# Loading only the right half of each Toeplitz band and copying its lower left quarter on VectorE

## The chip, the cores and the metric

The kernel runs on one core of a Trainium2 chip. The metric is the device time of one execution in microseconds (us); lower is better.

## What the kernel computes

`x` has shape batch 128, time 128, features 512; `cond` has shape 128 x 512. A causal convolution over time, whose taps are the rows of `cond`, is followed by a gated recurrence, and then by a tanh recurrence:

```python
x_pad = pad(x, K - 1 zeros in front of time)            # K = 128 taps
conv  = conv_b + sum(x_pad[:, k:k + L, :] * cond[k] for k in range(K))
proj  = conv @ Wp + bp
b_t, c_t = softplus(proj[..., :64]), tanh(proj[..., 64:])
u     = x @ Ws + bs
state = decay * state + dt * b_t * u_t                  # over time
x     = x + (c_t * state) @ Wo + bo
xW    = x @ Wx + b
h     = tanh(h @ Wh + xW_t)                             # 128 steps over time
out   = x + h
```

This case is about the convolution. For each of the 512 features it is a product of a 128 x 128 lower triangular Toeplitz matrix with that feature's 128 x 128 slice of `x`.

## The kernel before

**Stages.** The 512 features are worked off in KC = 4 chunks of P = 128. Each chunk has a convolution (`convolution`, one fp32 matmul per feature, 128 x 128 by 128 x 128) and then a projection (`projection`: transposes of the convolved tile and products with `Wp`). After the fourth chunk comes the recurrence over time, which takes the rest of the run. Within a chunk, four features share a PSUM bank (PER_BANK = 4), so a chunk fills BANKS = 32 banks in turn in the four banks CONV; ScalarE copies the even ones to SBUF and VectorE the odd ones (`copy_conv`), and TensorE may refill a bank only after its copy.

**The ring.** The matmul operands of CH = 8 features make one load, called here a group, so that a chunk has 16 groups and the kernel 64. Groups go to the RING = 8 slots of `t_ring` (the Toeplitz bands) and `x_ring` (the slices of `x`). The array `hankel` in HBM has each feature's taps once, behind zeros; the entry of a band at partition r and column l is `hankel[r + l]`, so a band is read with overlapping rows, a step of one tap from a partition to the next. Features lie in pairs (the last index of `t_ring`), so that one contiguous run of a partition is 512 B for 64 columns and 1024 B for all 128.

**The quarters of a band.** N = 64. Seen as partition halves by column halves: the upper left quarter (partitions 0 to 63, columns 0 to 63) is zero, which VectorE writes once per slot by memset. The upper right quarter is one DMA (`row, column = 0, N`: 64 partitions, 128 KB, 256 runs of 512 B); the lower half, left and right together, is a second (`N, 0`: 64 partitions, 256 KB, 256 runs of 1024 B). A third DMA brings `x_ring` (512 KB, 4 KB in each of 128 partitions). Since the entry depends on r + l alone, the lower left quarter has the same numbers as the upper right one.

**Order.** SyncE issues all loads, three DMAs per group on one queue (`load_ring`). It issues groups 0 to 7 at once, with the small loads of `vec`, `Wo` and `Ws` behind group 1 and `Wp` behind group 7. After that the load of group q + 8 waits until the matmuls of group q are done (`conv_done`). So the first eight groups of chunks 2 to 4 are loaded while the chunk before is convolved and projected, and their last eight during their own convolution. TensorE waits per group on the one semaphore `ring_loaded[slot]`, raised by all three DMAs. VectorE's program begins with the eight memsets, then scales vectors and `Wo` (waiting on their loads), and then runs `copy_conv` and the additions after the projections (`add_proj`) chunk by chunk. At the start ScalarE's first copy waits for GpSimd's work on the weights (`weights_ready`).

Of the kernel before, what the change touches and what calls it, by code (L numbers as in the profile page):

```python
# [12 lines left out]
TIME = 128  # L13
D = 512
N = 64
P = 128
KC = D // P
RING = 8
CH = 8
PER_BANK = 4  # L20
BANKS = P // PER_BANK
# [3 lines left out]
VECTORS = KC + 5  # L25
PAIRS = BANKS // 2
LAG = 3
LOAD = 3 * 16
DMA = 16

# [6 lines left out]
def build(nc, x_rev, x_dtb, hankel, h0_t, vectors, Wp, Ws, Wo, Wx, Wh, b, out):  # L38
# [6 lines left out]
    with ctx:  # L45
        def sb(stack, name, shape, dt=F32):
            return stack.enter_context(nc.sbuf_tensor(name, shape, dt))

        def sem(name):
            return ctx.enter_context(nc.semaphore(name))  # L50

        bank = [ctx.enter_context(nc.psum_tensor(f"bank{i}", [P, 512], F32)) for i in range(8)]
        CONV, TURN, PROJ = bank[0:4], bank[4:6] + bank[0:2], bank[2:4] + bank[6:8]
# [21 lines left out]
        with ExitStack() as first:  # L75

            t_ring = sb(first, "t_ring", [P, RING, CH // 2, TIME, 2])
            x_ring = sb(first, "x_ring", [P, RING, CH, BATCH])
            conv = sb(first, "conv", [P, TIME, P])  # L80
# [38 lines left out]
        def f(ap):  # L119
            return ap.bitcast(F32)  # L120

        ring_loaded = [sem(f"ring_loaded{i}") for i in range(RING)]
        t_zero = sem("t_zero")
        conv_done = sem("conv_done")
        conv_copied_act = sem("conv_copied_act")
        conv_copied_dve = sem("conv_copied_dve")
# [49 lines left out]
        def groups(engine, body):  # L176

            body(0, 0, True, False)
            body(1, 1, True, False)
            with engine.Fori(1, GROUPS // 2 - 1) as pair:  # L180
                body(2 * pair, 0, False, False)
                body(2 * pair + 1, 1, False, False)
            body(GROUPS - 2, 0, False, False)
            body(GROUPS - 1, 1, False, True)

        def toeplitz(row, column, n):

            return bass.AP(hankel.tensor, 2 * (row + column) + n * (CH // 2 * 4 * P),
                           [[2, N], [4 * P, CH // 2], [1, 2 * (TIME - column)]])

        block = ctx.enter_context(nc.Block())

        @block.sync
        def _(sp):
            def load_wp(c):
                rows = bass.ds(c * P, P)
                sp.dma_start(wp_now[:], Wp[rows, :]).then_inc(wp_loaded, DMA)  # L200

            def load_ring(n, slot):
                for row, column in ((0, N), (N, 0)):
                    sp.dma_start(t_ring[row:row + N, slot, :, column:, :].rearrange("p j l i -> p j (l i)"),  # L204
                                 toeplitz(row, column, n)).then_inc(ring_loaded[slot], DMA)
                sp.dma_start(x_ring[:, slot], x_rev[:, bass.ds(n * CH, CH), :]).then_inc(ring_loaded[slot], DMA)

            for n in range(RING):
                load_ring(n, n)
                if n == 1:  # L210
                    sp.dma_start(vec[:], vectors).then_inc(vec_loaded, DMA)
                    sp.dma_start(wo_f[0:N, :], Wo).then_inc(ws_wo_loaded, DMA)
                    sp.dma_start(ws_f, Ws.rearrange("(c p) n -> p c n", p=P)).then_inc(ws_wo_loaded, DMA)
            load_wp(0)
            per_chunk = P // CH
            with sp.Fori(0, KC - 1) as c:
                for q in range(per_chunk):

                    sp.wait_ge(conv_done, BANKS * c + CH // PER_BANK * (q + 1))
                    load_ring(per_chunk * c + q + RING, q % RING)  # L220
                    if q == per_chunk - 1:

                        sp.wait_ge(proj_done, BANKS * (c + 1))
                        load_wp(c + 1)
            for q in range(per_chunk - RING):
                sp.wait_ge(conv_done, BANKS * (KC - 1) + CH // PER_BANK * (q + 1))
                load_ring(per_chunk * (KC - 1) + q + RING, q % RING)

            sp.wait_ge(conv_done, BANKS * KC)  # L230
            sp.dma_start(w_f[:], Wx.rearrange("(c p) n -> p c n", p=P)).then_inc(wx_loaded, DMA)

            def load_x(g, slot):
                sp.dma_start(x_f[:, slot], x_dtb[:, bass.ds(g * G, G), :].rearrange("(c p) t b -> p c t b", p=P))\
                  .then_inc(x_loaded[slot], DMA)

            load_x(0, 0)
            sp.dma_start(b_rows[:], b.partition_broadcast(P)).then_inc(late_loaded, DMA)
            sp.dma_start(h0_f[:], h0_t.rearrange("(c p) b -> p c b", p=P)).then_inc(late_loaded, DMA)

            sp.wait_ge(weights_ready, 3)
            sp.dma_start(w_f[:], Wh.rearrange("(c p) n -> p c n", p=P)).then_inc(wh_loaded, DMA)

            sp.wait_ge(b_ready, BANKS - 2)
            sp.wait_ge(last_b_ready, 2)
            load_x(1, 1)

            def stores_and_loads(g, par, first, last):
                if not (last or (isinstance(g, int) and g == GROUPS - 2)):

                    sp.wait_ge(x1_ready, KC * (g + 1))
                    load_x(g + 2, par)

                for s in range(0, G, 1 if last else G):
                    n = 1 if last else G
                    sp.wait_ge(out_ready, G * g + s + n)
                    sp.dma_start(out[:, bass.ds(g * G + s, n), :].rearrange("(c p) t b -> p c t b", p=P),
                                 x1_f[:, par, :, s:s + n]).then_inc(stored[par], DMA)

            groups(sp, stores_and_loads)  # L260
            sp.wait_ge(stored[0], DMA * (GROUPS // 2))
            sp.wait_ge(stored[1], DMA * (GROUPS // 2 - 1 + G))
# [208 lines left out]
        def _(dve):  # L471
# [16 lines left out]
            nc.vector.tensor_scalar(rates[:, 1:2], rates[:, 0:1], -1.0, 1.0, ALU.mult, ALU.add).then_inc(rate_step, 1)  # L488
            decay = rates[N:P, 1:2]

            def copy_conv(c):
                with dve.Fori(0, BANKS // 4) as i:
                    m = 4 * i
                    for k in (1, 3):
                        dve.wait_ge(conv_done, BANKS * c + m + k + 1)
                        nc.vector.tensor_copy(conv[:, :, bass.ds((m + k) * PER_BANK, PER_BANK)],
                                              CONV[k][:].rearrange("p (d l) -> p l d", d=PER_BANK))\
                          .then_inc(conv_copied_dve, 1)

            def add_proj(c, m, k):  # L500
                dve.wait_ge(proj_done, BANKS * c + m + k + 1)
                cols = bass.ds((m + k) * 512, 512)
                nc.vector.tensor_tensor(bc[:, cols], PROJ[k][:], bc[:, cols], ALU.add).then_inc(proj_added, 1)  # L503

            copy_conv(0)
            with dve.Fori(0, BANKS // 4) as i:
                for k in range(4):
                    dve.wait_ge(proj_done, 4 * i + k + 1)
                    nc.vector.tensor_scalar(bc[:, bass.ds((4 * i + k) * 512, 512)], PROJ[k][:],  # L510
                                            bp_c[:, k % 2:k % 2 + 1], None, ALU.add).then_inc(proj_added, 1)
            with dve.Fori(1, KC - 1) as c:
                copy_conv(c)
                with dve.Fori(0, BANKS // 4) as i:
                    for k in range(4):
                        add_proj(c, 4 * i, k)

            copy_conv(KC - 1)

            def soft_abs_even(q, slot):
# [115 lines left out]
        def _(pe):  # L637
            pe.wait_ge(ident_ready, 1)

            def convolution(c):  # L640

                for d in range(P):
                    slot, m = (d // CH) % RING, d // PER_BANK
                    if d % CH == 0:
                        pe.wait_ge(t_zero, slot + 1)
                        pe.wait_ge(ring_loaded[slot], LOAD * (P // CH // RING) * c + LOAD * (d // CH // RING + 1))
                    if d % PER_BANK == 0 and m >= 4:  # L650

                        if m % 2 == 0:
                            pe.wait_ge(conv_copied_act, BANKS // 2 * c + (m - 4) // 2 + 1)
                        else:
                            pe.wait_ge(conv_copied_dve, BANKS // 2 * c + (m - 4) // 2 + 1)
                    mm = nc.tensor.matmul(CONV[m % 4][:, bass.ts(d % PER_BANK, TIME)], x_ring[:, slot, d % CH],  # L656
                                          t_ring[:, slot, d % CH // 2, :, d % 2], start=True, stop=True)
                    if d % PER_BANK == PER_BANK - 1:
                        mm.then_inc(conv_done, 1)
# [20 lines left out]
            with pe.Fori(0, KC - 1) as c:  # L680
                convolution(c)
                projection(c)

                pe.wait_ge(proj_added, BANKS * (c + 1) - 2)
# [136 lines left out]
```

## Time and profile before

| | |
|---|---|
| time, median of 3 runs | 1267.18 us (1267.06 to 1269.96) |
| the profiled execution's own time | 1265.97 us |
| its span | 1264.2 us |
| TensorE busy | 1187.3 us (94%) |
| VectorE busy | 657.2 us (52%) |
| share of the 16 DMA engines taken by the one load and store queue | 37.5% |
| TensorE's mean granted clock | 0.98 |

The span runs from the first to the last instruction of the profiled execution, and its own time holds in addition what lies around it. Busy shares are means over stages that differ: the four convolutions and projections fill the first 307 us, the recurrence the rest.

### The profile page before, as it was taken

How to read it: one execution, taken by the hardware profiler on the slowest of the kernel's cores; microseconds unless marked ns; L12 is line 12 of the kernel's file. 1: busy time of each engine (PE TensorE's matmuls, PEld its weight loads, DVE VectorE, ACT ScalarE, POOL GpSimd, SP SyncE). 2: the span in 40 equal slices, each digit the busy share in tenths (PEclk: the TensorE clock that was granted, in tenths of full speed). 3: DMA queues.
4: the chain of work that ended last, by engine and by line, in shares of the span. 5: the costliest groups of instructions: out<-in, count | busy, mean ns of one | idle time of the engine just before them, and what ended most of it. 6: DMA issues, size and time to landing. Idle time of an engine off the chain costs nothing.

```text
span 1264.2 us, 17115 instructions
## 1 busy us (share of the span) xinstructions
PE 1187.3 (94%) x5888; PEld 950.0 (75%) x5888; DVE 657.2 (52%) x1022; ACT 504.6 (40%) x756; POOL 333.4 (26%) x179
## 2 busy tenths in 40 slices
PE   4589899998859999999999999999999999999997
PEld 4567758677427888888888888888888888888886
DVE  2135354443996555555554555555555555455553
ACT  1144352443664434344433344443434443334432
POOL 1000000001433443333443333344333344333330
PEclk9899999998889999999999999999999999999999
DMA  9994968938102223222223222222322222322201
GB/s 215 222 216 109 273 145 212 257 98 223 34 0 67 68 91 105 71 66 66 66 69 104 92 66 66 66 66 94 100 71 66 66 66 73 106 87 66 66 34 67
DMA packets 82485, 129.54 MB, mean 102 GB/s; under 512 B 4960, under 2 KB 40800, under 8 KB 82464
## 3 DMA queue, kind: packets, MB, share of 16 engines
q1 hardware_dynamic: 82464, 129.26, 37.5%
q8 instruction: 13, 0.21, 0.1%
q14 instruction: 8, 0.07, 0.0%
HBM read 95.69 MB, written 33.55 MB: 102 GB/s over the span
## 4 chain that ended last, share of the span: by engine, by line
PE 84%; SPq 5%; DVE 4%; DMA 3%; issue 2%; ACT 0%; POOL 0%; DVEq 0%; POOLq 0%; ACTq 0%
PE bank L725 9%; PE bank L733 9%; PE bank L734 9%; PE bank L719 9%; PE bank L718 9%; PE bank L737 9%; PE bank L677 7%; PE bank L656 5%; PE bank L761 4%; PE bank L669 4%; DMA x_ring<-x_rev 3%; SPq L204 3%; PE bank L708 2%; PE bank L709 2%; PE bank L700 2%
## 5 line engine op out<-in xcount | busy, mean ns | idle before, releaser
L324 POOL TENSOR_TENSOR x_lo<-x_f,x_hi 128x512 fp32r<-128x512 f32 x126 | 160.2, 1307 | 556.0 <-ACT x_hi L442 556.0
L453 ACT ACTIVATE h_f<-z_f 128x512 f32<-128x512 f32 x128 | 80.9, 632 | 346.6 <-DVE z_f L612 346.6
L616 DVE TENSOR_TENSOR hT_lo<-bank,hT_hi 128x512 fp32r<-128x512 f32 x128 | 88.5, 691 | 216.1 <-ACT hT_hi L457 216.1
L733 PE MATMUL bank<-wh_hi,hT_hi 128*128 128x512 f32 x512 | 200.5, 392 | 0.0
L734 PE MATMUL bank<-wh_lo,hT_hi 128*128 128x512 f32 x512 | 200.0, 391 | 0.0
L719 PE MATMUL bank<-wx_lo,x_hi 128*128 128x512 f32 x512 | 199.7, 390 | 0.0
L718 PE MATMUL bank<-wx_hi,x_hi 128*128 128x512 f32 x512 | 199.5, 390 | 0.0
L656 PE MATMUL bank<-t_ring,x_ring 128*128 128x128 f32 x1024 | 134.7, 292 | 44.9 <-DMA x_ring<-x_rev 36.2
L656 PEld LDWEIGHTS bank<-t_ring,x_ring 128*128 128x128 f32 x1024 | 128.7, 202 | 52.1 <-issue 38.5
L612 DVE TENSOR_TENSOR z_f<-bank,b_rows 128x512 f32<-128x512 f32 x128 | 88.5, 691 | 132.4 <-PE bank L737 128.5
L318 POOL TENSOR_TENSOR x_lo<-x_f,x_hi 128x2048 fp32r<-128x2048 f32 x32 | 147.9, 4621 | 21.8 <-PE bank L669 21.8
L725 PE MATMUL bank<-wx_hi,x_lo 128*128 128x512 f32 x512 | 144.6, 404 | 0.4 <-POOL x_lo L324 0.4
L677 PE MATMUL bank<-turned,wp_now 128*128 128x512 f32 x256 | 134.4, 615 | 10.9 <-DVE bc L503 10.2
L737 PE MATMUL bank<-wh_hi,hT_lo 128*128 128x512 f32 x512 | 136.9, 389 | 0.0
L733 PEld LDWEIGHTS bank<-wh_hi,hT_hi 128*128 128x128 f32 x512 | 96.1, 188 | 26.0 <-ACT hT_hi L457 6.2
L457 ACT CAST hT_hi<-bank 128x512 fp32r<-128x512 f32 x128 | 75.1, 587 | 94.7 <-PE bank L761 94.7
L669 PEld LDWEIGHTS bank<-ident,conv 128*128 128x128 f32 x512 | 63.4, 142 | 64.7 <-issue 64.7
L718 PEld LDWEIGHTS bank<-wx_hi,x_hi 128*128 128x128 f32 x512 | 96.2, 188 | 20.4 <-ACT x_hi L442 0.4
L737 PEld LDWEIGHTS bank<-wh_hi,hT_lo 128*128 128x128 f32 x512 | 96.1, 188 | 20.2
L719 PEld LDWEIGHTS bank<-wx_lo,x_hi 128*128 128x128 f32 x512 | 96.2, 188 | 20.0
L734 PEld LDWEIGHTS bank<-wh_lo,hT_hi 128*128 128x128 f32 x512 | 96.2, 188 | 19.7
L442 ACT CAST x_hi<-x_f 128x512 fp32r<-128x512 f32 x128 | 79.6, 622 | 77.2 <-DVE x_f L589 75.0
(67 smaller groups left out, 1418.0 us busy)
## 6 DMA issues: line engine op xcount, KB each, us to landing
x_ring<-x_rev SPq DMA_DIRECT2D x64, 512.0 KB, 12.5
x_f<-x_dtb SPq DMA_DIRECT2D x32, 1024.0 KB, 8.1
out<-x_f SPq DMA_DIRECT2D x31, 1024.0 KB, 5.3
t_ring<-hankel SPq DMA_DIRECT2D x64, 256.0 KB, 11.7
t_ring<-hankel SPq DMA_DIRECT2D x64, 128.0 KB, 11.1
w_f<-Wx SPq DMA_DIRECT2D x1, 1024.0 KB, 5.4
w_f<-Wh SPq DMA_DIRECT2D x1, 1024.0 KB, 5.0
out<-x_f SPq DMA_DIRECT2D x4, 256.0 KB, 2.3
```

The source lines that it names most:

```text
L318: nc.gpsimd.tensor_tensor(x_lo[:], x_f[:, par], f(x_hi[:]), ALU.subtract).then_inc(xlo_ready, 1)
L324: nc.gpsimd.tensor_tensor(x1_lo[:, c], x1_f[:, par, c], f(x1_hi[:, c]), ALU.subtract)\
L612: nc.vector.tensor_tensor(z_f[:], ZB[s % 2][:], b_rows[:], ALU.add).then_inc(zsum_ready, 1)
L656: mm = nc.tensor.matmul(CONV[m % 4][:, bass.ts(d % PER_BANK, TIME)], x_ring[:, slot, d % CH], t_ring[:, slot, d % CH // 2, :, d % 2], star ...
L669: mm = nc.tensor.transpose(TURN[m % 4][:, bass.ts(i, P)], conv[:, m * PER_BANK + i], ident[:])
L677: nc.tensor.matmul(PROJ[n % 4][:], wp_now[:, bass.ts(n % 2, P)], turned[:, n % 4], start=True, stop=True)\
L718: nc.tensor.matmul(z, x1_hi[:, k, s], wx_hi[:, k], start=(k == 0), stop=False)
L719: nc.tensor.matmul(z, x1_hi[:, k, s], wx_lo[:, k], start=False, stop=False)
L725: mm = nc.tensor.matmul(z, x1_lo[:, k, s], wx_hi[:, k], start=False, stop=stop and k == KC - 1)
L733: nc.tensor.matmul(z, hT_hi[:, k], wh_hi[:, k], start=False, stop=False)
L734: nc.tensor.matmul(z, hT_hi[:, k], wh_lo[:, k], start=False, stop=False)
L737: mm = nc.tensor.matmul(z, hT_lo[:, k], wh_hi[:, k], start=False, stop=stop and k == KC - 1)
```

## The change

Of each band only the right half (all 128 partitions, columns 64 to 127) is loaded, in one DMA of 256 KB with 512 runs of 512 B. VectorE then copies the upper right quarter (64 partitions, 4 x 128 numbers in each) into the lower left one (`fill_band`), once for each of the 64 groups. The upper left quarter stays the memset one. The shared semaphore is split in three: `t_loaded[slot]` (the band's DMA, waited for by VectorE), `xr_loaded[slot]` (waited for by TensorE) and `t_full` (raised by the copy, waited for by TensorE). In `copy_conv` VectorE copies the band of group n + 1 ahead of the odd bank of group n, and the band of the next chunk's first group stands behind the last bank.

```diff
-LOAD = 3 * 16
-        ring_loaded = [sem(f"ring_loaded{i}") for i in range(RING)]
+        t_loaded = [sem(f"t_loaded{i}") for i in range(RING)]
+        xr_loaded = [sem(f"xr_loaded{i}") for i in range(RING)]
+        t_full = sem("t_full")
...
-        def toeplitz(row, column, n):
-            return bass.AP(hankel.tensor, 2 * (row + column) + n * (CH // 2 * 4 * P),
-                           [[2, N], [4 * P, CH // 2], [1, 2 * (TIME - column)]])
+        def band(n):
+            return bass.AP(hankel.tensor, 2 * N + n * (CH // 2 * 4 * P), [[2, P], [4 * P, CH // 2], [1, 2 * N]])
...
             def load_ring(n, slot):
-                for row, column in ((0, N), (N, 0)):
-                    sp.dma_start(t_ring[row:row + N, slot, :, column:, :].rearrange("p j l i -> p j (l i)"),
-                                 toeplitz(row, column, n)).then_inc(ring_loaded[slot], DMA)
-                sp.dma_start(x_ring[:, slot], x_rev[:, bass.ds(n * CH, CH), :]).then_inc(ring_loaded[slot], DMA)
+                sp.dma_start(t_ring[:, slot, :, N:, :].rearrange("p j l i -> p j (l i)"), band(n))\
+                  .then_inc(t_loaded[slot], DMA)
+                sp.dma_start(x_ring[:, slot], x_rev[:, bass.ds(n * CH, CH), :]).then_inc(xr_loaded[slot], DMA)
...
+            def fill_band(c, n):
+                slot = n % RING
+                dve.wait_ge(t_loaded[slot], DMA * (P // CH // RING) * c + DMA * (n // RING + 1))
+                nc.vector.tensor_copy(t_ring[N:P, slot, :, 0:N, :].rearrange("p j l i -> p j (l i)"),
+                                      t_ring[0:N, slot, :, N:, :].rearrange("p j l i -> p j (l i)")).then_inc(t_full, 1)
+
             def copy_conv(c):
-                with dve.Fori(0, BANKS // 4) as i:
-                    m = 4 * i
-                    for k in (1, 3):
-                        dve.wait_ge(conv_done, BANKS * c + m + k + 1)
-                        nc.vector.tensor_copy(conv[:, :, bass.ds((m + k) * PER_BANK, PER_BANK)],
-                                              CONV[k][:].rearrange("p (d l) -> p l d", d=PER_BANK))\
-                          .then_inc(conv_copied_dve, 1)
+                for n in range(P // CH):
+                    if n + 1 < P // CH:
+                        fill_band(c, n + 1)
+                    m = 2 * n + 1
+                    dve.wait_ge(conv_done, BANKS * c + m + 1)
+                    nc.vector.tensor_copy(conv[:, :, bass.ts(m, PER_BANK)],
+                                          CONV[m % 4][:].rearrange("p (d l) -> p l d", d=PER_BANK))\
+                      .then_inc(conv_copied_dve, 1)
...
+            fill_band(0, 0)
             copy_conv(0)
+            fill_band(0, P // CH)
...
             with dve.Fori(1, KC - 1) as c:
                 copy_conv(c)
+                fill_band(c, P // CH)
...
                     if d % CH == 0:
                         pe.wait_ge(t_zero, slot + 1)
-                        pe.wait_ge(ring_loaded[slot], LOAD * (P // CH // RING) * c + LOAD * (d // CH // RING + 1))
+                        pe.wait_ge(t_full, P // CH * c + d // CH + 1)
+                        pe.wait_ge(xr_loaded[slot], DMA * (P // CH // RING) * c + DMA * (d // CH // RING + 1))
```

SyncE's program where its loop over the later loads begins, before the change (one group is the rows from one `conv_done` wait to the next; `t_ring` is the band, `x_ring` the slice of `x`):

```order
L204 ISA [waits conv_done]
L204 DMA t_ring<-hankel 64x4x128
L204 DMA t_ring<-hankel 64x4x256
L206 ISA
L206 DMA x_ring<-x_rev 128x1024
L219 REGISTER_ALU
```

The same place now:

```order
L200 ISA [waits conv_done]
L200 DMA t_ring<-hankel 128x4x128
L202 ISA
L202 DMA x_ring<-x_rev 128x1024
L215 REGISTER_ALU
```

Two issues per group stand where there were three.

VectorE's program behind the memsets, before the change (`turned` holds `Wo` here, `bank` is a convolution bank):

```order
L484 TENSOR_SCALAR turned<-turned,rates_e 64x512 [waits ws_wo_loaded]
L486 TENSOR_SCALAR turned<-turned,rates_e 64x512 [waits wo_scaled]
L488 TENSOR_SCALAR rates<-rates 128x1 [waits rate_step]
L492 UNCONDITIONAL_BRANCH
L492 ISA
L496 ISA [waits conv_done]
L496 COPY conv<-bank 128x128x4
```

The same place now:

```order
L480 TENSOR_SCALAR turned<-turned,rates_e 64x512 [waits ws_wo_loaded]
L482 TENSOR_SCALAR turned<-turned,rates_e 64x512 [waits wo_scaled]
L484 TENSOR_SCALAR rates<-rates 128x1 [waits rate_step]
L491 COPY t_ring<-t_ring 64x4x128 [waits t_loaded0]
L491 COPY t_ring<-t_ring 64x4x128 [waits t_loaded1]
L500 COPY conv<-bank 128x128x4 [waits conv_done]
L491 COPY t_ring<-t_ring 64x4x128 [waits t_loaded2]
L500 COPY conv<-bank 128x128x4 [waits conv_done]
```

The first band copy, on which TensorE's first matmul now waits, stands behind the scaling of `Wo`; from there on a band copy and a bank copy alternate.

VectorE's program at the end of the first chunk's convolution, now (before, the wait on `proj_done` followed the last bank copy directly):

```order
L500 COPY conv<-bank 128x128x4 [waits conv_done]
L491 COPY t_ring<-t_ring 64x4x128 [waits t_loaded7]
L500 COPY conv<-bank 128x128x4 [waits conv_done] x2
L491 COPY t_ring<-t_ring 64x4x128 [waits t_loaded0]
L513 UNCONDITIONAL_BRANCH
L513 ISA
L516 ISA [waits proj_done]
L516 TENSOR_SCALAR bc<-bank,vec 128x512
```

The band copy of the next chunk's first group now stands ahead of the first addition behind a projection.

## Rows read from the trace of the kernel before

**Rows 1.** The four convolutions as windows: length, busy us per engine, clock, DMA share.

```profile
core 0: us, PE busy (x) PEld busy (x) DVE busy (x) ACT busy (x) POOL busy (x), PEclk, DMA share, GB/s
8.45:74.27 65.82, 41.48 (x256) 38.06 (x256) 11.91 (x21) 9.68 (x18) 2.94 (x4) 0.87 1.09 225
116.76:151.34 34.58, 30.31 (x257) 29.35 (x256) 11.33 (x17) 9.37 (x16) 0.00 (x0) 1.00 0.97 244
193.83:227.39 33.56, 29.98 (x257) 29.22 (x256) 11.21 (x17) 9.37 (x16) 0.00 (x0) 1.00 0.96 251
269.89:307.04 37.15, 32.93 (x257) 31.70 (x255) 11.21 (x17) 9.36 (x16) 0.00 (x0) 0.91 0.83 202
```

**Rows 2.** TensorE's waits, 0 to 380 us: who for whom, total, times, longest.

```profile
PE bank L656 <- DMA x_ring<-x_rev: 36.2, 20, 8.5
```

**Rows 3.** TensorE's timeline, first convolution: start, length, what, idle before and releaser.

```profile
8.45 6.05 PE L656 MATMUL bank<-t_ring,x_ring 128*128 128x128 f32 x32 [8.45 <-DMA x_ring<-x_rev]
18.81 5.60 PE L656 MATMUL bank<-t_ring,x_ring 128*128 128x128 f32 x32 [4.31 <-ACT conv L357]
...
29.82 2.08 PE L656 MATMUL bank<-t_ring,x_ring 128*128 128x128 f32 x16 [1.88 <-DMA x_ring<-x_rev]
...
72.19 2.08 PE L656 MATMUL bank<-t_ring,x_ring 128*128 128x128 f32 x16 [2.23 <-DMA x_ring<-x_rev]
```

**Rows 4.** The same timeline, second and third convolution.

```profile
139.09 2.08 PE L656 MATMUL bank<-t_ring,x_ring 128*128 128x128 f32 x16 [0.33 <-DMA x_ring<-x_rev]
...
149.26 2.08 PE L656 MATMUL bank<-t_ring,x_ring 128*128 128x128 f32 x16 [1.32 <-DMA x_ring<-x_rev]
...
193.83 23.76 PE L656 MATMUL bank<-t_ring,x_ring 128*128 128x128 f32 x208
```

**Rows 5.** The same timeline, last convolution.

```profile
290.82 2.06 PE L656 MATMUL bank<-t_ring,x_ring 128*128 128x128 f32 x16 [0.82 <-issue]
...
298.85 5.90 PE L656 MATMUL bank<-t_ring,x_ring 128*128 128x128 f32 x32 [1.05 <-issue]
```

**Rows 6.** SyncE's issues, second convolution: start, length, DMAs.

```profile
120.57 0.45 SPq L206 DMA_DIRECT2D x_ring<-x_rev  x1
...
148.54 1.30 SPq L204 DMA_DIRECT2D t_ring<-hankel  x2
150.03 1.43 SPq L206 DMA_DIRECT2D x_ring<-x_rev  x1
151.74 1.30 SPq L204 DMA_DIRECT2D t_ring<-hankel  x2
```

**Rows 7.** DMAs: KB, us to landing; issued at 120.57, from 148.54, at 151.74.

```profile
x_ring<-x_rev SPq DMA_DIRECT2D x1, 512.0 KB, 4.8
...
x_ring<-x_rev SPq DMA_DIRECT2D x1, 512.0 KB, 12.5
t_ring<-hankel SPq DMA_DIRECT2D x1, 256.0 KB, 11.7
t_ring<-hankel SPq DMA_DIRECT2D x1, 128.0 KB, 11.1
...
t_ring<-hankel SPq DMA_DIRECT2D x1, 128.0 KB, 11.3
```

**Rows 8.** VectorE groups, 0 to 380 us: form, count | busy, mean ns | idle.

```profile
L496 DVE COPY conv<-bank 128x512 f32 x64 | 44.1, 691 | 120.5 <-PE bank L656 120.5
L563 DVE COPY s_f<-v_f 64x128 f32<-64x128 f32 x1 | 1.2, 1209 | 0.0
L484 DVE TENSOR_SCALAR turned<-turned,rates_e 64x512 f32<-64x512 f32 x1 | 0.7, 704 | 0.0
L486 DVE TENSOR_SCALAR turned<-turned,rates_e 64x512 f32<-64x512 f32 x1 | 0.5, 479 | 0.0
```

**Rows 9.** VectorE's timeline around the second convolution's start.

```profile
114.50 3.33 DVE L510 TENSOR_SCALAR bc<-bank,vec 128x512 f32 x4 [0.55 <-PE bank L677]
118.97 0.69 DVE L496 COPY conv<-bank 128x512 f32 x1 [1.15 <-PE bank L656]
```

## Prediction

> **What bounds the kernel now.** I first split the run into stages, because the change touches the loads of the four convolutions alone. Their windows [rows 1] last 65.8, 34.6, 33.6 and 37.2 us and hold the same 128 fp32 matmuls each. In all four the DMA engines are busy nearly throughout (share 0.83 to 1.09), VectorE for about 11 us. Next I asked what TensorE waits for: within the first 380 us 36.2 us of its idle time end with the landing of `x_ring`, the third DMA of a load [rows 2]. The timeline of TensorE shows the shape. In the first convolution, from group 5 on, each group waits for its own load: groups 5 and 15 start at 29.82 and 72.19 [rows 3], so the pace is 42.37 / 10 = **4.24 us per load**. In the second convolution it is (149.26 - 139.09) / 3 = **3.39 us** at the end [rows 4], in the last one (298.85 - 290.82) / 2 = **4.0 us** [rows 5]. Where the operands lie ready TensorE needs 23.76 us for 13 groups [rows 4], **1.83 us per group**, hence 16 x 1.83 + 0.2 for the tail = **29.5 us** for a convolution. So the convolutions are bound by their loads, the first wholly, the others in their second half, and 29.5 us is the floor under each.
>
> **What the change removes.** Each load shrinks from 896 KB to 768 KB and from three issues to two. How much time that is depends on which of the two band DMAs cost it. In a backlog, landings follow each other as the queue is worked off [rows 6, 7]. Of the load issued from 148.54 the 128 KB DMA lands at 148.54 + 11.1 = 159.6, the 256 KB one, issued half of 1.30 us later, at 149.2 + 11.7 = 160.9, `x_ring` at 150.03 + 12.5 = 162.5; the next 128 KB one lands at 151.74 + 11.3 = 163.0. So the three take about 0.5, 1.3 and 1.6 us, together 3.4, which is the pace just found. The 256 runs of 512 B take 0.5 us and the 256 runs of 1024 B 1.3: more than twice the time for twice the bytes. No row shows 512 B runs to all 128 partitions in one DMA. Its price is bounded by the nearest rows: at `x_ring`'s bytes per time 256 / 512 x 1.6 = 0.8 us; at the small DMA's price per run 2 x 0.5 = 1.0; at both band DMAs' bytes per time 1.8 x 256 / 384 = 1.2; at the larger one's price per run 2 x 1.3 = 2.6. I take 1.0, since runs of just this length have that row. A load then takes **2.65 us** where it took 3.4.
>
> A rule stands beside that price. The Trainium skill, SBUF — State Buffer, section Door 1, has partitions 0 to 63 on eight of SBUF's sixteen DMA ports and 64 to 127 on the other eight, so each old band DMA had half the ports and the new one has all. From its ceiling of 435 GB/s for all ports I estimate 0.6 us for the 128 KB DMA and 1.2 for the 256 KB one; the rows' 0.5 and 1.3 agree. By that rule the new DMA would take 0.6 us instead of my 1.0, a load 2.25, and the sum below would be 37 us instead of 31.8, or 1230 us.
>
> **First convolution.** Its loads go at 4.24 us, 1.26 times as slow as in the second for the same bytes. If that factor stays the new pace is 2.65 x 1.26 = 3.35; if it comes from the two half-width DMAs getting in each other's way, it goes and the pace is 2.65. Nothing in the rows decides, and I take the middle, **3.1 us**. The bounds are 2.65 and, by bytes alone, 4.24 x 768 / 896 = 3.63. Between the first load and the sixteenth lie 15 of them: 15 x (4.24 - 3.1) = **17.1 us** saved.
>
> **The other convolutions.** Here the last eight loads are issued during the convolution. In the second, which starts at 116.76, `x_ring` of the first such load is issued at 120.57 and lands 4.8 us later [rows 6, 7], 8.6 us into the convolution; with one issue less, some 7.5. Seven more follow, then the last group's 2.1 us: 7.5 + 7p + 2.1 for a pace p. At the old pace, with 8.6, that gives 8.6 + 23.7 + 2.1 = 34.4, against 34.58 in the row. At p = 2.65 it gives 28.2, below the floor of 29.5, so TensorE becomes the bound and the second and third convolution save 34.6 - 29.5 = **5.1** and 33.6 - 29.5 = **4.1 us**. The last one has lost more: its later loads come at 4.0 us. Its mean pace from the same formula is (37.15 - 2.1 - 8.6) / 7 = 3.8; times 2.65 / 3.4 this is 3.0, so 7.5 + 21 + 2.1 = 30.6, saving **6.5 us**.
>
> **What the change adds.** 64 copies on VectorE of 64 partitions x 512 fp32, SBUF to SBUF. The trace has no such copy. The nearest rows are `Wo`'s scalings of the same shape: 479 ns in place, 704 ns from the lower to the upper partitions [rows 8]; a fourfold smaller copy with 1209 ns is the upper bound. I take 0.6 us. Per group VectorE then has 0.69 (a bank copy, [rows 8]) + 0.6 = 1.3 of TensorE's 1.83 us, and the copies hide twice: behind `x_ring`, which lands 1.6 us after the band where loads bound, and behind the previous group's matmuls where TensorE bounds. That cover is gone if a copy takes over 1.83 - 0.69 = 1.14 us; at 1209 ns each of up to 64 groups would cost 0.07 us, some 4 us at most.
>
> Two places need a look because VectorE runs in order. At each later convolution's start the copy for its second group stands behind the last additions, which end at 114.50 + 3.33 = 117.83 [rows 9]; the copy ends at 118.4, and the second group is due at 116.76 + 1.83 = 118.59: no stall, but only 0.2 us of slack. At each convolution's end the copy for the next chunk's first group stands ahead of the additions. Its band lands about 1 us after the last `x_ring`, before the last group's matmuls are over, and the first addition of the chunk cannot start until a projection product is done. At the very start the first copy stands behind the scaling of `Wo`, so TensorE starts at about 15.5 instead of 8.45 [rows 3]. It then had to wait anyway, for ScalarE until 18.81 with two groups done; those two groups took it 6.05 us, and with the later start I expect group 2 at 20 to 21.5. From there it gains on loads that come every 3.1 us and has caught up by group 7. Cost on the path: nothing, and 2 us if the pace is near 2.65. For all of this together I charge 1 us.
>
> **Sum.** 17.1 + 5.1 + 4.1 + 6.5 - 1 = 31.8 us. The profiled execution took 1265.97, so it would be 1234.2; the median of the runs is 1.2 us higher, so I forecast **1235 us**. The projections and the recurrence only move earlier.
>
> **Rivals.**
> *A. The loads stop binding everywhere (chance 0.25).* The two half-width DMAs are what makes the queue slow, and full-width loads run at 2.65 us or below in the first convolution too. For it: the slow factor of 1.26 has no other visible cause. Against: `x_ring`, full width already, is most of a load. First convolution: 15 x (4.24 - 2.65) = 23.9, less 2 for the late start; last one at the floor, 7.7. With 5.1 and 4.1 this is 38.8 saved, 1228 us. If the pace falls to 2.4, the first gives 27.6 less 2, and 1225. The port rule named above speaks for this rival too: transfers that each use all ports have no half to crowd.
>
> *B. Bytes alone count, at each stage's old rate (0.20).* First 15 x (4.24 - 3.63) = 9.1; the others at paces 2.9, 2.9 and 3.26: 29.9, 29.9 and 32.4 us, saving 4.7, 3.7 and 4.7. Together 22, less 1: 1246 us. For it: the rates differ between stages though the mix does not.
>
> *C. Runs alone count (0.05).* A load has 256 + 256 + 128 runs before and 512 + 128 after. If a run's price doesn't hang on its length, nothing is saved and the copies are hidden: 1267 us. Against: 0.5 against 1.3 us for 256 runs.
>
> *D. Slower (0.06).* The place is the band's DMA: 512 runs at the 1024 B run's price take 2.6 us where both old ones took 1.8, 0.8 more per load. First: 15 x 0.8 x 1.26 = 15 us; the other three 7 x 0.8 = 5.6 each. Together 32, so 1299 us. It decides once the new DMA takes over 1.8 us, 1.8 times my price. Against: half of those runs are exactly the old small DMA, at 0.5.
>
> **How the numbers follow.** My forecast with paces between A and B has 0.44. The range is 1223 to 1250: A and B with their bounds lie inside, C and D outside, and so do mixes such as B with slow copies. Differences within 0.3% (3.8 us) cannot be told from none by a measurement of this kernel. C is the same, with a little of D's milder form: 0.05. D gives slower, 0.05. The rest is faster, 0.90.
>
> **What would show it.** In the new profile the third step is right if the first convolution's groups start 3.1 us apart, from 2.65 (A) to 3.6 (B). The second and third convolution should last 29.5 to 30 us with no wait for `x_ring`, the last 29.5 to 32.5. The band copies should show 0.48 to 0.70 us, with TensorE hardly ever released by them. VectorE's busy time should grow by 64 x 0.6 = 38 us. The band's DMA should land about 1.6 us ahead of `x_ring`; a gap near zero would expose the copy. The prediction fails if the band's DMA takes clearly more than 1.2 us, if TensorE's waits move onto the copies, or if TensorE's granted clock falls to half during a projection, which happened in convolutions with gaps (mean 0.87 and 0.91, [rows 1]) and not in those without.

## The result and the profile after

The change makes the kernel faster: 1217.54 us (1216.49 to 1217.91) against 1267.12 us (1265.07 to 1269.96), a ratio of 0.9599 with a 95% interval of 0.9547 to 0.965. The prediction was 1235 us with a range of 1223 to 1250. The sign was right, but the measured time lies below the range: the gain was 49.6 us instead of 32. The kernel before was timed again with each set of experiments: medians 1266.69 and 1265.00 us, single runs from 1258.67 to 1274.13. It varies more than the changed kernel, whose four runs lie within 1.5 us.

The four convolutions of the changed kernel as windows (length, busy us per engine, granted clock, DMA share, GB/s), beside [rows 1]:

```profile
core 0: us, PE busy (x) PEld busy (x) DVE busy (x) ACT busy (x) POOL busy (x), PEclk, DMA share, GB/s
12.03:43.51 31.48, 31.26 (x256) 30.67 (x256) 16.98 (x30) 9.37 (x16) 1.85 (x2) 1.00 1.07 360
86.03:115.37 29.34, 29.29 (x257) 29.09 (x256) 17.47 (x32) 9.36 (x16) 0.00 (x0) 1.00 0.94 314
157.74:186.99 29.25, 29.25 (x257) 29.06 (x256) 17.53 (x32) 9.37 (x16) 0.00 (x0) 1.00 0.95 314
229.36:258.54 29.18, 29.18 (x257) 28.98 (x255) 17.53 (x32) 9.37 (x16) 0.00 (x0) 1.00 0.67 221
```

The first convolution ends at 43.51 us instead of 74.27, the others last 29.2 to 29.3 us instead of 34.6, 33.6 and 37.2. That is 30.8 + 5.2 + 4.3 + 8.0 = 48.3 of the 49.5 us by which the span fell (1264.2 to 1214.7). In the first convolution the DMA engines moved 360 GB/s, up from 225.

The granted clock is at its upper level (2.4 GHz) in all four, where the first and last had means of 0.87 and 0.91, so the clock could be a second cause of the gain. The old rows speak against it. In the kernel before, first convolution:

```profile
46.37 3.78 PE L656 MATMUL bank<-t_ring,x_ring 128*128 128x128 f32 x16 [1.22 <-DMA x_ring<-x_rev]
50.72 2.08 PE L656 MATMUL bank<-t_ring,x_ring 128*128 128x128 f32 x16 [0.57 <-DMA x_ring<-x_rev]
```

The group at 46.37 ran at a granted clock of 0.51, that is at the lower level (1.2 GHz), and took 3.78 us instead of 2.08. The next group still had to wait 0.57 us for its load.

TensorE's timeline shows each convolution as one long row. Against [rows 3 to 5] the waits for single loads are gone:

```profile
12.03 31.48 PE L664 MATMUL bank<-t_ring,x_ring 128*128 128x128 f32 x256 [12.03 <-DVE t_ring L491]
...
86.09 29.28 PE L664 MATMUL bank<-t_ring,x_ring 128*128 128x128 f32 x256
...
157.74 29.25 PE L664 MATMUL bank<-t_ring,x_ring 128*128 128x128 f32 x256
...
229.36 29.18 PE L664 MATMUL bank<-t_ring,x_ring 128*128 128x128 f32 x256
```

The first is still 2.2 us longer than the others. The chain of waits shows its last two groups at the pace of the loads, 2.18 us apart instead of 1.83:

```profile
39.27 2.06 PE bank L664 x16
41.33 0.13 issue
41.45 2.05 PE bank L664 x16
```

The trace has the landings of `x_ring` for these groups at 39.2 and 41.4 us.

TensorE's waits up to 340 us (compare [rows 2]):

```profile
PE bank L664 <- DVE t_ring L491: 12.0, 1, 12.0
```

VectorE's groups up to 380 us (count, then busy us in all and mean ns of one), the bank copy and the new band copy:

```profile
L500 DVE COPY conv<-bank 128x512 f32<-128x512 f32 x64 | 44.3, 691 | 47.5 <-PE bank L664 47.5
L491 DVE COPY t_ring<-t_ring 64x512 f32<-64x512 f32 x64 | 27.8, 435 | 2.1
```

The 64 copies take 435 ns in the mean. After the first, TensorE is never released by one.

To see what a load costs, take SyncE's issues of one load and the next, issued while TensorE finishes the first convolution and landing after it:

```profile
38.59 0.38 SPq L200 DMA_DIRECT2D t_ring<-hankel  x1
39.18 1.04 SPq L202 DMA_DIRECT2D x_ring<-x_rev  x1
40.48 0.59 SPq L200 DMA_DIRECT2D t_ring<-hankel  x1
41.26 1.08 SPq L202 DMA_DIRECT2D x_ring<-x_rev  x1
```

and their times from issue to landing (first load, then the next):

```profile
x_ring<-x_rev SPq DMA_DIRECT2D x1, 512.0 KB, 9.1
t_ring<-hankel SPq DMA_DIRECT2D x1, 256.0 KB, 7.9
...
x_ring<-x_rev SPq DMA_DIRECT2D x1, 512.0 KB, 9.2
t_ring<-hankel SPq DMA_DIRECT2D x1, 256.0 KB, 8.6
```

The landings are 46.5 (band), 48.3 (`x_ring`), 49.1, 50.5. So the second load's band takes 0.8 us and its `x_ring` 1.4, a load **2.2 us**. The 1.8 us between the first two landings is an exception: for the loads issued at 20.70 and 24.48 the trace has the band and `x_ring` landing at 29.1 and 30.5, and at 33.5 and 34.8, two loads in 4.3 us. Read the same way, [rows 6, 7] gave 0.5 + 1.3 + 1.6 = 3.4, and the first convolution's pace was 4.24.

### The profile page after: what moved, and what is told of

Read it like the earlier page. It is cut to its first block, busy times and chain, and to the rows that moved or that the text cites. A ratio compares the mean times of both kernels' runs of the same rounds, so it can differ in the third digit from the quotient of the medians.

```text
span 1214.7 us, 16920 instructions
## 1 busy us (share of the span) xinstructions
PE 1170.6 (96%) x5888; PEld 939.4 (77%) x5888; DVE 685.1 (56%) x1086; ACT 504.8 (42%) x756; POOL 333.7 (27%) x179
## 4 chain that ended last, share of the span: by engine, by line
PE 93%; DVE 3%; issue 1%; DMA 0%; ACT 0%; POOL 0%; DVEq 0%; SPq 0%; POOLq 0%
PE bank L664 10%; PE bank L733 10%; PE bank L741 10%; PE bank L742 10%; PE bank L745 9%; PE bank L727 9%; PE bank L726 9%; PE bank L685 8%; PE bank L769 5%; PE bank L677 4%; PE bank L716 2%; PE bank L717 2%; PE bank L702 2%; PE bank L708 2%; DVE bc L539 1%
## 5 line engine op out<-in xcount | busy, mean ns | idle before, releaser
L664 PE MATMUL bank<-t_ring,x_ring 128*128 128x128 f32 x1024 | 119.0, 276 | 12.3 <-DVE t_ring L491 12.0
L664 PEld LDWEIGHTS bank<-t_ring,x_ring 128*128 128x128 f32 x1024 | 118.0, 190 | 14.6 <-issue 14.6
```

## The experiments

**What made the loads slow.** The load shrank by 14% in bytes and its time by 35% (from 3.4 us) to 48% (from 4.24). The theory that I formed from this: a DMA over partitions 0 to 63 or 64 to 127 alone is slow and also slows what runs beside it (width theory). The rivals: bytes, length of a run, number of DMAs. Four kernels tell them apart.

*Whole band in one full-width DMA*, more bytes than ever and no copy:

```diff
-                for row, column in ((0, N), (N, 0)):
-                    sp.dma_start(t_ring[row:row + N, slot, :, column:, :].rearrange("p j l i -> p j (l i)"),
-                                 toeplitz(row, column, n)).then_inc(ring_loaded[slot], DMA)
+                sp.dma_start(t_ring[:, slot].rearrange("p j l i -> p j (l i)"), band(n)).then_inc(ring_loaded[slot], DMA)
```

> The kernel before with the whole band in one DMA over all 128 partitions (512 KB, 512 runs of 1024 B, the zero quarter read from the zeros of hankel), no copy and no memset. A load has 1024 KB, more than before (896) and after (768). Width theory (what made the loads slow is that each old band DMA reached only half of the partitions): loads run at the changed kernel's bytes per time, 768 KB in 2.2 us, so 2.9 us each; the first convolution ends near 52 us instead of 74, the others near their floor; 1228 us (1222 to 1236). Bytes theory: 4.24 x 1024 / 896 = 4.85 us per load in the first convolution, total 1280 to 1290 us. Run length theory (1024 B runs are the dear ones): 2.6 + 1.3 = 3.9 us per load, 1250 to 1262 us.

Measured: 1231.12 us, a ratio of 0.9711 (0.9653 to 0.977) to the kernel before. Consecutive groups of the first convolution:

```profile
48.77 2.08 PE L653 MATMUL bank<-t_ring,x_ring 128*128 128x128 f32 x16 [0.71 <-DMA x_ring<-x_rev]
51.57 2.08 PE L653 MATMUL bank<-t_ring,x_ring 128*128 128x128 f32 x16 [0.72 <-DMA x_ring<-x_rev]
```

1024 KB in 2.8 us, where 896 KB took 4.24: the width theory's number, and neither rival's. Bytes and run length can't be what held the loads back. They are not without effect once every DMA is full width: with 256 KB less per load the changed kernel is another 13.6 us faster.

*The right half in two DMAs of 64 partitions*, in the changed kernel:

```diff
-                sp.dma_start(t_ring[:, slot, :, N:, :].rearrange("p j l i -> p j (l i)"), band(n))\
-                  .then_inc(t_loaded[slot], DMA)
+                for row in (0, N):
+                    sp.dma_start(t_ring[row:row + N, slot, :, N:, :].rearrange("p j l i -> p j (l i)"),
+                                 bass.AP(hankel.tensor, 2 * (row + N) + n * (CH // 2 * 4 * P),
+                                         [[2, N], [4 * P, CH // 2], [1, 2 * N]])).then_inc(t_loaded[slot], DMA)
```

> The changed kernel with the right half in two DMAs of 64 partitions each, 128 KB each: same bytes, same runs, same copies, one issue more. Width theory: the load is slower again, 2.7 to 3.3 us instead of 2.2, the first convolution ends some 10 us later, 1228 us (1223 to 1237). Bytes theory and run length theory: as the changed kernel, 1218 us (1215 to 1220).

*Its control, two DMAs of all partitions, half of the feature pairs each*:

```diff
+                for j in (0, CH // 4):
+                    sp.dma_start(t_ring[:, slot, j:j + CH // 4, N:, :].rearrange("p j l i -> p j (l i)"),
+                                 bass.AP(hankel.tensor, 2 * N + n * (CH // 2 * 4 * P) + j * 4 * P,
+                                         [[2, P], [4 * P, CH // 4], [1, 2 * N]])).then_inc(t_loaded[slot], DMA)
```

> The control: the changed kernel with the right half in two DMAs of all 128 partitions, each two of the four feature pairs, 128 KB each. Same bytes, runs, copies and number of issues as the run with two half-width DMAs. Width theory: 1218 us (1215 to 1220). A theory by which the number of DMAs counts (three issues per load instead of two): the same as the run with two half-width DMAs, both above 1222 us.

Measured: halves by partitions 1243.81 us (1242.97 to 1248.13), halves by features 1218.29 us (1217.94 to 1219.07). Bytes, runs, number of DMAs and copies are equal; 25.5 us hang on the width alone. The page of each has (count, KB each, median us from issue to landing), for the run with half widths and then for its control:

```profile
x_ring<-x_rev SPq DMA_DIRECT2D x64, 512.0 KB, 10.9
...
t_ring<-hankel SPq DMA_DIRECT2D x128, 128.0 KB, 9.2
```

```profile
x_ring<-x_rev SPq DMA_DIRECT2D x64, 512.0 KB, 7.6
...
t_ring<-hankel SPq DMA_DIRECT2D x128, 128.0 KB, 6.5
```

Over a first convolution the half-width run moved 243 GB/s, its control 360 GB/s. The windows, half widths first:

```profile
14.66:60.03 45.37, 33.89 (x256) 31.99 (x256) 16.98 (x30) 9.37 (x16) 1.85 (x2) 1.00 1.09 243
```

```profile
12.27:44.19 31.92, 31.79 (x256) 31.44 (x256) 17.00 (x30) 9.38 (x16) 1.87 (x2) 1.00 1.07 360
```

The effect is larger than I expected of it (1228 us, 1223 to 1237). A third issue per load costs next to nothing (1218.29 against 1217.54 us).

*Bytes as before, but only the lower left quarter half-width*:

```diff
-                for row, column in ((0, N), (N, 0)):
+                for row, column, height in ((0, N, P), (N, 0, N)):
+                    sp.dma_start(t_ring[row:row + height, slot, :, column:column + N, :].rearrange("p j l i -> p j (l i)"),
+                                 part(row, column, height, n)).then_inc(ring_loaded[slot], DMA)
```

> The kernel before with its 384 KB per band cut otherwise: the right half over all 128 partitions (256 KB) and the lower left quarter over 64 (128 KB), all runs of 512 B; bytes as before, three issues as before, no copy on VectorE. Width theory: most of the band is full width, so the load takes 2.6 to 3.5 us, 1238 us (1225 to 1250). Bytes theory: as before, 1267 us. Run length theory: 768 runs of 512 B at 0.5 us per 256 are 1.5 us instead of 1.8, pace 3.9 in the first convolution, 1258 us.

Measured: 1259.84 us (1255.4 to 1266.52), a ratio of 0.9953 (0.9915 to 0.999). This missed: I had expected the full-width part to carry the time to 1238 us. One half-width DMA of 128 KB among 896 KB keeps most of the loss, and the number alone fits the run length theory's 1258 as well. The load doesn't: its pace in the first convolution is 3.24 us (rows below), within the 2.6 to 3.5 of the width theory and not the other's 3.9. What I got wrong was what such a pace costs over the four convolutions. The run length theory had also fallen with the full-band run; the next run shows what the time does hang on.

**Which partitions.** *The same kernel with the 64-partition DMA moved to partitions 32 to 95*:

```diff
-                for row, column, height in ((0, N, P), (N, 0, N)):
+                for row, column, height in ((0, N, P), (N // 2, 0, N)):
```

> The run with the right half over 128 partitions and a 64-partition quarter beside it, with one edit: that 128 KB DMA goes to partitions 32 to 95 instead of 64 to 127 (same size, runs and number of issues). The lower left quarter is then wrong in partitions 96 to 127 and the upper left not zero in 32 to 63, so the output isn't the reference's. 
Measured: 1226.95 us (1226.5 to 1227.97). 33 us lie between the medians of two kernels that differ in which 64 partitions a 128 KB DMA writes. (Two things go along with it: its source begins 32 taps earlier, and VectorE's memset of the zero quarter is split in two, 32 partitions each, to leave 32 to 95 free.) The kept profiles are 27.4 us apart, 10.0 of it in the first convolution and the rest in the other three, which last 36.1, 36.7 and 34.4 us at 64 to 127 and 29.4, 29.4 and 30.6 at 32 to 95. The first convolutions of the run at 64 to 127 and of the run at 32 to 95, as windows:

```profile
6.68:61.68 55.00, 39.33 (x256) 36.82 (x256) 11.92 (x21) 9.67 (x18) 2.95 (x4) 0.91 1.10 280
```

```profile
7.48:51.71 44.23, 36.09 (x256) 34.13 (x256) 14.56 (x27) 9.67 (x18) 2.95 (x4) 0.96 1.09 343
```

and two consecutive groups of each, in the same order:

```profile
56.36 2.08 PE L660 MATMUL bank<-t_ring,x_ring 128*128 128x128 f32 x16 [1.19 <-DMA x_ring<-x_rev]
59.60 2.08 PE L660 MATMUL bank<-t_ring,x_ring 128*128 128x128 f32 x16 [1.16 <-DMA x_ring<-x_rev]
```

```profile
47.01 2.08 PE L661 MATMUL bank<-t_ring,x_ring 128*128 128x128 f32 x16 [0.55 <-DMA x_ring<-x_rev]
49.63 2.08 PE L661 MATMUL bank<-t_ring,x_ring 128*128 128x128 f32 x16 [0.54 <-DMA x_ring<-x_rev]
```

The pace is 3.24 us against 2.62, with every byte, run and issue equal. A DMA of 64 partitions is not slow in itself; at 64 to 127 it is, and at 32 to 95 it is not. This is what the Trainium skill, SBUF — State Buffer, section Door 1, says: bit 6 of the partition number chooses between the even and the odd ports, so 32 to 95 reach all sixteen and 64 to 127 only eight. These runs agree with it. The ports themselves are seen in no trace, and partitions 0 to 63 were not tried alone.

Next, does the half-width DMA slow what runs beside it? The transfer rate between 20 and 40 us, in slices of 0.5 us, again at 64 to 127 and then at 32 to 95:

```profile
GB/s 338 325 306 205 186 238 381 334 321 266 188 198 303 370 330 324 209 167 256 356 334 326 320 249 202 227 346 347 310 309 222 216 313 351 341 291 265 202 313 376
```

```profile
GB/s 359 333 327 358 349 373 339 331 343 342 381 358 360 309 331 366 383 322 351 331 350 382 346 334 327 335 392 355 340 319 361 346 368 346 330 341 352 388 325 346
```

Once per load the first falls to about 200 GB/s for 1 to 1.5 us, in which 200 to 300 KB go through (an estimate from the slices), more than the 128 KB of the DMA at 64 to 127. The second stays level. The packet records of the same 20 us tell whose packets these are. A packet of 4096 B belongs to `x_ring` and goes to one partition. It takes 232 ns in the mean at 64 to 127 and 177 at 32 to 95; 265 ns in the run with two halves and 178 in its control; 261 in the kernel before and 177 in the changed one. So the untouched `x_ring` is slowed by the half-width DMAs beside it.

**Are the copies and the late start on the path?** The chain of the changed kernel's profile leads from the first convolution back through the first band copy and the scaling of `Wo` to the load of `vec`:

```profile
2.81 5.97 DMA vec<-vectors
...
9.86 0.58 DVE turned L480
...
10.46 0.48 DVE turned L482
...
11.03 0.87 DVE t_ring L491
```

*No copies at all*; the lower left quarter stays zero (a memset of all partitions), so part of the convolution is left out, and TensorE waits for the band's DMA itself:

```diff
-                nc.vector.memset(t_ring[0:N, slot, :, 0:N, :], 0.0).then_inc(t_zero, 1)
+                nc.vector.memset(t_ring[:, slot, :, 0:N, :], 0.0).then_inc(t_zero, 1)
...
-                        pe.wait_ge(t_full, P // CH * c + d // CH + 1)
+                        pe.wait_ge(t_loaded[slot], DMA * (P // CH // RING) * c + DMA * (d // CH // RING + 1))
```

> The changed kernel without VectorE's copies: the lower left quarter stays zero by a memset of all partitions, so the convolution is wrong; TensorE waits for the band's DMA itself. Theory (the copies are hidden, and the first convolution's end at 43.5 us is set by the landing of its sixteenth load, not by TensorE's start at 12.0): within 1 us of the changed kernel, 1217 us (1216 to 1219). Rival (the late start behind the scaling of Wo is on the path): TensorE starts at 5 to 6 us, and 3 to 6 us are saved, 1212 to 1214 us.

*The first two band copies ahead of the scaling, ScalarE's wait for the weights behind its bank copies*:

```diff
+            for n in range(2):
+                fill_band(0, n)
...
-            act.wait_ge(weights_ready, 2)
             with act.Fori(0, KC - 1) as c:
                 copy_conv(c)
+                act.wait_ge(weights_ready, 2)
```

> The changed kernel with the first two band copies ahead of the scaling of vectors and Wo on VectorE, and ScalarE's wait for the weights moved behind its first bank copies, so that TensorE can start at about 6 us and run on. Theory (the first convolution is bound by its loads up to the last): 1217 us (1215 to 1219). Rival (start on the path): 1211 to 1214 us.

Measured: 1218.30 us (1217.45 to 1218.67) and 1217.98 us (1217.85 to 1218.57), no less than the changed kernel's 1217.54. The copies cost nothing, and nor does starting TensorE 6 us later. Their timelines begin so, without copies and then with the early start:

```profile
5.50 5.73 PE L659 MATMUL bank<-t_ring,x_ring 128*128 128x128 f32 x32 [5.50 <-DMA x_ring<-x_rev]
14.97 28.65 PE L659 MATMUL bank<-t_ring,x_ring 128*128 128x128 f32 x224 [3.74 <-ACT conv L353]
```

```profile
5.77 5.88 PE L666 MATMUL bank<-t_ring,x_ring 128*128 128x128 f32 x32 [5.77 <-DVE t_ring L475]
...
35.54 8.56 PE L666 MATMUL bank<-t_ring,x_ring 128*128 128x128 f32 x64 [0.16 <-issue]
```

Started at 5.50, 5.77 and 12.03 us, the first convolution ends at 43.62, 44.10 and 43.51. Without copies TensorE still stood 3.74 us behind ScalarE's first bank copy, so it is the second run that tests the early start. TensorE gets no further than its loads. The chain named the start because TensorE's gaps are tiny (0.13 us at 41.33) and it names no load as their cause, which is no evidence that an earlier start would help.

**How much cover the copies have.** *Each band copy three times in a row*:

```diff
+                for k in range(3):
+                    if k:
+                        dve.wait_ge(t_full, 3 * (P // CH) * c + 3 * n + k)
```

> The changed kernel with each band copy made three times, one behind the other. The cover that the prediction named is 1.14 us per group beside the bank copy of 0.69 us. Three copies of 0.42 us with a handoff of about 0.06 between them are some 1.4 us, so VectorE needs 2.1 us per group against TensorE's 1.83, and becomes the bound: 16 x 0.27 = 4 us in each of three convolutions and 0 to 2 in the first, whose loads come every 2.2 us: 1231 us (1226 to 1237). Rival (the copies have more cover than that, since copies can run ahead): under 1220 us.

Measured: 1240.51 us (1239.61 to 1241.18), 23 us more. VectorE in the second convolution:

```profile
97.52 0.69 DVE L503 COPY conv<-bank 128x512 f32<-128x512 f32 x1
98.24 1.33 DVE L494 COPY t_ring<-t_ring 64x512 f32<-64x512 f32 x3
99.68 0.69 DVE L503 COPY conv<-bank 128x512 f32<-128x512 f32 x1
```

The period is 2.16 us per group where TensorE alone needs 1.83, so VectorE is the bound, as the prediction's limit of 1.14 us says: the copies take 1.33 here. The period is 0.14 us more than the copies' 0.69 + 1.33, so the limit is rather 1.0 us than 1.14. 16 x 0.33 = 5.3 us in each of four convolutions is 21 of the 23 us. This missed too (1231 us, 1226 to 1237): I had reckoned with three convolutions and 0.27 us.

## Why the prediction missed

**What bounds the kernel now** was right. The three windows that now run at 29.2 to 29.3 us confirm the floor of 29.5. What the prediction says of the clock, that it fell in the convolutions with gaps and not in those without, is not quite what [rows 1] show: the second had gaps too, at 1.00.

**What the change removes** was mis-sized. The band's new DMA takes 0.8 us, not 1.0, at the lower of the bounds. As large an error was to leave `x_ring` at 1.6 us because the change does not touch it. It takes 1.4 now: part of what rows 6 and 7 put down to `x_ring` was the half-width DMAs beside it. In all a load takes 2.2 us instead of 2.65. The port rule gave 2.25, partly by luck: its band was 0.6 us, which is too short, and its `x_ring` the same old 1.6, which is too long. The 37 us that the prediction puts beside it doesn't follow from its own steps either. With 0.4 us less per load the first convolution alone saves 6 us more, and the last one reaches its floor, which makes 39, or 1228 us.

**The first convolution** is the step that failed. I named the two half-width DMAs getting in each other's way as the possible cause of its pace of 4.24 us, said that no row decides, and took 3.1, the middle of the bounds 2.65 and 3.63. The cause was right and the middle was not: 2.2 us is below even the lower bound of 2.65, since the bound kept the faster stage's landings, in which the same crowding was at work. The term was 17.1 us and measured 30.8. Fifteen intervals at 2.2 instead of 4.24 would give 30.6, but that agreement is in part luck. The first `x_ring` lands at 5.2 us instead of 8.4, and the sixteenth at 41.4 where it landed at 72.2. So 3.2 us come from the first landing, which the prediction left where it was, and 27.6 from the fifteen intervals, which take 2.4 us in the mean, with the small loads of `vec`, `Wo`, `Ws` and `Wp` among them. Rival A had the cause, at a chance of 0.25, and still reached only 1225 to 1228 us: it too ended at 2.4 us per load, and it took off 2 us for the late start. The port rule stood beside my sum as a price for the band's own DMA, and beside rival A as an argument; its effect on `x_ring` got no price anywhere.

**The other convolutions**: 5.1, 4.1 and 6.5 us predicted, 5.2, 4.3 and 8.0 measured. The last one missed by the same error of pace: it reached the floor.

**What the change adds**: hidden, as predicted. The copy takes 0.42 us in most cases, below the row of 479 ns that I took as nearest from below, not 0.6. The 1 us that I charged, and the 2 us for the late start in rival A, were not lost. TensorE started at 12.03, not 15.5, because the small loads landed earlier too (VectorE is released by `vec` at 8.8 us instead of 12.7), and its start doesn't matter.

In sum 30.8 + 5.2 + 4.3 + 8.0 = 48.3. Of the other 1.2 us of the span 1.0 lie behind the fourth convolution (956.2 us instead of 957.1). The same stretch takes 956.8 to 957.6 us in the traces of the other runs, so this looks like spread.

**Rival B** (bytes alone) and **C** (runs alone) are refuted by the full-band run: more bytes and as many runs per load (512 + 128), and 36 us faster than before. **D** needed a band DMA over 1.8 us and found 0.8.

What stays open is by what way a half-width DMA slows its neighbours, and why the kernel before kept a pace of 4.24 us in the first convolution and 3.39 in the second for the same load. The packet records say only where the time is: the 4096 B packets of the kernel before take 261 ns between 20 and 40 us and 220 between 125 and 145, against 177 in the changed kernel, so the crowding was there in both stages and worse in the first.

## What to carry to other kernels

Where loads bound a kernel, look at which partitions each DMA writes before counting its bytes: here 1024 KB per load over all partitions beat 896 KB in halves by 36 us. Cut a tile along its free dimension, not at partition 64, and rather load a quarter of zeros than leave it out at that price. A copy on an engine with idle time is free as long as it fits beside that engine's other work in the period of the engine that bounds; and a DMA that is slow in a backlog slows what is queued with it, so the price of an untouched neighbour is not a constant (here a 4096 B packet of `x_ring`, 261 ns and then 177).

## What was unexpected

A single 128 KB DMA to partitions 64 to 127 in each 896 KB load cost 33 us over the kernel against the same DMA to partitions 32 to 95. With full-width DMAs only, the queue kept 360 GB/s with runs of 512 B and 4 KB. With the whole band in runs of 1024 B it kept 368 GB/s over the first convolution:

```profile
6.46:53.65 47.19, 36.60 (x256) 34.00 (x256) 11.90 (x21) 9.67 (x18) 2.95 (x4) 0.96 1.06 368
```
